# Second layer: skip product on TensorE, y read by ScalarE, the low half of u made by GpSimd and placed by transfers

## The chip, the cores and the metric

The kernel runs on one core of one Trainium2 chip. The metric is the device time of the whole program in microseconds (us); smaller is better. The number to forecast is the median of several runs.

## What is computed

Two layers on an image batch x of shape (4, 128, 64, 64), float32. The first layer is attention over the 4096 pixels with 4 heads, residual and layer norm. The second layer adds three branches of its input: a 3x3 convolution, a linear map in the Fourier plane, and a Mamba block. The change touches the Mamba block alone:

```python
xs = jax.nn.silu((xc + conv1d_b[None, :, None]).transpose(0, 2, 1))
x_dbl = jnp.einsum('bld,rd->blr', xs, x_proj_w)
dt = jax.nn.softplus(jnp.einsum('blr,dr->bld', x_dbl[..., :DT_RANK], dt_proj_w) + dt_proj_b)
...
dA = jnp.exp(dtt[..., None] * A)
h = dA * h + dtt[..., None] * Bt[:, None, :] * xt[..., None]
y = jnp.einsum('bdn,bn->bd', h, Ct)
...
return ys.transpose(1, 0, 2) + x * D
...
y = y * jax.nn.silu(z)
```

There are 256 channels d, 16 states n and 4096 positions l. The last sum, `+ x * D`, is called the skip below, and `dt * xs` is called u.

## The kernel before

`layer0` runs first and writes its result to the DRAM tensor `z_ext`; `layer1` reads it. The engines of `layer1` each run their own list of instructions in order, and semaphores tie them together.

**Tiling.** `layer1` walks over 32 items (4 images x 8 stretches of 512 positions). An item has 32 groups g; a group is 8 channels x 16 states on 128 partitions, over 512 positions. Each engine has an `emit(it, p)` that loops over the groups g of item `it`, and inside each step calls `prepare(it + 1, ...)`, which does a piece of the next item's preparation at a fixed g. So the order is written out by hand by the numbers g.

**One group.** SyncE (SP) loads dt of the group's channels, repeated over the states, into one of 16 buffers `d_a` (L885); ScalarE (ACT) makes the decay exp(dt*A) in it (L1119). TensorE (PE) repeats u over the states with a 0/1 matrix into one of 4 PSUM banks (`repeat_u`, L1021); VectorE (DVE) multiplies this by B (`times_b`, L1181) and runs the recurrence (the scan, L1195) into one of 8 buffers `hh`; ACT keeps the last state (`last_state`, L1112); GpSimd (POOL) multiplies by C into one of 8 buffers `hc` (L1232). After each four groups PE sums the states into the bank of y (`sum_states`, L1004, four matmuls side by side on 32 columns each). Sixteen groups fill one half of y, 128 channels.

**How far the engines may run apart.** PE may do `repeat_u` of group g once scan g - 4 is done, and DVE multiplies it after scan g - 2. ACT makes the decay of group g + 1 after keeping the state of group g - 6. The scan of g waits for POOL's product and ACT's copy of g - 8. Loads of dt run 16 groups ahead.

**y.** DVE reads a finished half of y from PSUM, adds the skip and writes `yt` (`add_skip`, L1166, at g = 21 for half 0 and g = 5 of the next item for half 1). POOL multiplies by the gate (L1215), PE projects (`out_proj`, L1011, at g = 12 and 13), ACT copies the output bank (L1138), DVE adds a row (L1172) and SP stores.

**Preparation of the next item.** TensorE: taps at g = 1 to 7 (L939), `wxd` at 10 and 11, dt at 14 and 15, B and C at 18 and 19, gate at 22 and 23 (L966), the eight products with `wmix` at 29 (L973, L974), and the convolution's products at the g of `FILLS` (L986). ScalarE: softplus pieces at g = 17 to 20. GpSimd: dt's sum at g = 18 (L1220), u at g = 19 (L1223); SP stores dt at its step 16 and reads it back from there. The matmul of u runs in one pass, so u is split: ScalarE copies a rounded high half of 64 partitions into the stack `s_u` (L1064, g = 23 and 24, with the two partition halves one after the other), and DVE writes u minus this into the other 64 partitions (`low`, L1154, g = 23 and 24).

## Time and profile before

| | us |
|---|---|
| median of 3 runs | 5988.45 |
| lowest, highest | 5988.19, 5989.36 |
| the profiled execution, its own time | 5988.07 |
| its span, first to last instruction | 5986.3 |

| engine | busy us | share of the span |
|---|---|---|
| PE (matmul) | 5515.8 | 92% |
| DVE | 4841.2 | 81% |
| POOL | 4207.8 | 70% |
| ACT | 3701.3 | 62% |

How to read it: busy times are sums over both layers, which have different limits, so the second layer has to be read by itself. It fills the time from about 4000 us on. Matmuls overlap in the records, so a busy PE is not a full one. A row of the timeline gives start, duration, engine, line, operation, output and inputs, and in square brackets how long the engine had been idle and who ended that.

### The profile page before, as it was taken

The numbers are of one execution on the slowest core, as the hardware profiler recorded it, in microseconds if no ns is written. First come the engines' busy times: TensorE is split into PE (matmuls) and PEld (weight loads), VectorE is DVE, ScalarE is ACT, GpSimd is POOL, SyncE is SP. The second block draws the span as 40 slices with busy tenths as digits, with TensorE's granted clock in tenths as the row PEclk, the third lists the DMA queues.
The fourth block names the chain that finished last, engine by engine and source line by source line (L and its number), as shares of the span: only waits on it lengthen the run. The fifth ranks groups of instructions, "written<-read, shape, count | busy, mean of one in ns | idle before, by whom it ended". The sixth has DMA issues, their size and how long they took to land. (4 is left out here: it accounts for less than half of the span.)

```text
span 5986.3 us, 84041 instructions
## 1 busy us (share of the span) xinstructions
PE 5515.8 (92%) x27184; PEld 2520.1 (42%) x27184; DVE 4841.2 (81%) x7122; ACT 3701.3 (62%) x7290; POOL 4207.8 (70%) x3213
## 2 busy tenths in 40 slices
PE   7999999999999999999999999968888878888887
PEld 4444444444444444444444444423333333333333
DVE  7777777777777777777777777639999999999999
ACT  3666666665666666666666666656666666666665
POOL 2767666677676677776667776638787887878787
PEclk8999999999999999999999999989999999999999
DMA  4011010110110101101010000024444444454444
GB/s 135 21 43 41 20 38 22 43 40 27 43 35 21 45 20 43 41 24 36 24 26 22 8 22 13 20 94 172 168 161 168 160 169 162 168 168 160 168 160 153
DMA packets 292503, 464.74 MB, mean 78 GB/s; under 512 B 72384, under 2 KB 95808, under 8 KB 290624
## 3 DMA queue, kind: packets, MB, share of 16 engines
q1 hardware_dynamic: 292064, 459.37, 23.6%
q8 instruction: 217, 3.56, 0.2%
q14 instruction: 222, 1.82, 0.1%
HBM read 381.41 MB, written 76.28 MB: 76 GB/s over the span
## 5 line engine op out<-in xcount | busy, mean ns | idle before, releaser
L560 POOL TENSOR_TENSOR sums<-exps 128x512 f32<-128x512 f32 x2048 | 2617.2, 1298 | 1313.2 <-ACT exps L493 1308.3
L569 DVE TENSOR_REDUCE mpart<-ps 128x1 f32<-128x512 f32 x4096 | 2541.6, 683 | 818.9 <-PE ps L369 818.9
L493 ACT ACTIVATE exps<-ps 128x512 f32<-128x512 f32 x4096 | 2127.9, 603 | 1404.0 <-PE ps L376 1403.6
L369 PE MATMUL ps<-k_st,q_ring 96*128 96x512 f32 x4096 | 1753.9, 429 | 17.3 <-DMA k_st<-qk_split 8.9
L1232 POOL TENSOR_TENSOR hc<-hh,c_rep 128x512 f32<-128x512 f32 x1024 | 1361.8, 1338 | 392.3 <-DVE hh L1195 391.9
L376 PE MATMUL ps<-q_ring,k_st 98*128 98x512 f32 x4096 | 1621.7, 397 | 4.0 <-ACT exps L493 3.6
L1195 DVE TENSOR_TENSOR_SCAN hh<-d_a,carry,ps 128x512 f32<-128x512 f32 x1024 | 1308.6, 1281 | 1.0
L369 PEld LDWEIGHTS ps<-k_st,q_ring 96*128 96x128 f32 x4096 | 775.1, 189 | 1063.4 <-DVE mpart L569 508.2
L387 PE MATMUL ps<-exps,v_ring 128*32 128x512 f32 x8192 | 1090.8, 605 | 0.0
L376 PEld LDWEIGHTS ps<-q_ring,k_st 98*128 98x128 f32 x4096 | 777.7, 190 | 148.4 <-ACT exps L493 17.3
L1021 PE MATMUL ps<-s_u,sel_g 128*128 128x512 f32 x1024 | 559.1, 549 | 199.0 <-DVE hh L1195 197.4
L1119 ACT ACTIVATE d_a<-d_a,a_neg 128x512 f32<-128x512 f32 x1024 | 730.8, 720 | 3.6 <-DMA d_a<-dt_dram 2.0
L1181 DVE TENSOR_TENSOR ps<-ps,b_rep 128x512 f32<-128x512 f32 x1024 | 700.8, 687 | 12.6 <-PE ps L1021 11.6
L1021 PEld LDWEIGHTS ps<-s_u,sel_g 128*128 128x128 f32 x1024 | 194.7, 191 | 870.0 <-DVE hh L1195 752.8
L399 PE MATMUL ps<-sums,ones_d 128*32 128x512 f32 x4096 | 533.1, 592 | 0.0
L1004 PE MATMUL ps<-hc,sel_y 128*32 128x512 f32 x2048 | 287.2, 633 | 183.6 <-DVE yt L1166 114.7
L387 PEld LDWEIGHTS ps<-exps,v_ring 128*32 128x32 f32 x8192 | 161.2, 108 | 416.9 <-ACT exps L493 361.2
L1112 ACT COPY carry<-hh 128x1 f32<-128x1 f32 x1024 | 186.7, 183 | 238.8 <-DVE hh L1195 238.5
L939 PE MATMUL ps<-za,wtap 128*128 128x512 f32 x528 | 266.0, 598 | 27.2 <-DMA stage_j<-z_ext 27.2
L986 PE MATMUL ps<-zp,wconv 128*128 128x512 f32 x576 | 290.0, 604 | 0.0
L399 PEld LDWEIGHTS ps<-sums,ones_d 128*32 128x32 f32 x4096 | 133.0, 110 | 306.6 <-issue 298.1
L1064 ACT CAST s_u<-ux 64x1024 fp32r<-64x1024 f32 x66 | 68.9, 1045 | 286.0 <-POOL ux L1223 285.2
(106 smaller groups left out, 3075.4 us busy)
## 6 DMA issues: line engine op xcount, KB each, us to landing
d_a<-dt_dram SPq DMA_DIRECT2D x1040, 256.0 KB
qk_split<-hilo SPq DMA_DIRECT2D x128, 256.0 KB, 2.3
q_ring<-qk_split SPq DMA_DIRECT2D x384, 64.0 KB, 2.0
k_st<-qk_split SPq DMA_DIRECT2D x45, 512.0 KB, 7.1
dt_dram<-dt SPq DMA_DIRECT2D x33, 512.0 KB, 2.8
za<-z_ext SPq DMA_DIRECT2D x33, 320.0 KB, 3.8
zp<-z_ext SPq DMA_DIRECT2D x32, 320.0 KB, 6.6
xc<-in_x SPq DMA_DIRECT2D x32, 256.0 KB, 3.0
```

The costliest lines, as they stand in the source:

```text
L369: nc.tensor.matmul(d_bank(("max", m, t)), q_ring[0:PARTS, m % 4, 128 * i:128 * i + 128], k_st[0:PARTS, g % 2, chunk(kc)], start=True, stop ...
L376: nc.tensor.matmul(a_bank(("exp", n, t)), k_st[0:SHIFT, n // NCH % 2, 128 * t:128 * t + 128], q_ring[0:SHIFT, n % 4, :], start=True, stop= ...
L387: ins = nc.tensor.matmul(ps[D * i:D * i + D, OUT_BANK, :], v_ring[:, n // NCH % 2, 4 * v + i, :], exps[:, (2 * v + i // 2) % 4, CH * (i % ...
L399: nc.tensor.matmul(ps[D * j:D * j + D, DEN_BANK, :], ones_d[:, :], sums[:, u % 8, :], start=(v == 1), stop=(v == QUADS - 1)).then_inc(sum_ ...
L493: nc.scalar.activation(exps[:, u % 4, CH * half:CH * half + CH], a_bank(("exp", n, t)), ACT.Exp, scale=SCALE).then_inc(a_done, 1)
L560: pool.tensor_tensor(sums[:, u % 8, :], exps[:, u % 4, 0:CH], exps[:, u % 4, CH:2 * CH], ALU.add).then_inc(summed, 1)
L569: nc.vector.tensor_reduce(mpart[:, m % 2, t % 4, t // 4:t // 4 + 1], d_bank(("max", m, t)), AX.X, ALU.max).then_inc(d_done, 1)
L1021: nc.tensor.matmul(ps[:, U_BANK + g % NU, :], sel_g[:, j, :], s_u[:, p, s, :], start=True, stop=True).then_inc(u_rep, 1)
L1119: nc.scalar.activation(d_a[:, g % NDA, :], d_a[:, g % NDA, :], ACT.Exp, scale=a_neg[:, s * 8 + j:s * 8 + j + 1]).then_inc(da_ready, 1)
L1181: nc.vector.tensor_tensor(bu, bu, b_rep[:, p, :], ALU.mult).then_inc(bu_ready, 1)
L1195: nc.vector.tensor_tensor_scan(hh[:, g % NHH, :], d_a[:, g % NDA, :], ps[:, U_BANK + g % NU, :], carry[:, it % STEPS, s * 8 + j:s * 8 + j ...
L1232: pool.tensor_tensor(hc[:, g % NHC, :], hh[:, g % NHH, :], c_rep[:, p, :], ALU.mult).then_inc(hc_ready, 1)
```

## The change

In the second layer:

- **Skip.** DVE's `add_skip` is gone. A diagonal matrix of D (`wskip`, loaded once more with the weights) is multiplied with `xs` on PE as the first matmul into the bank of y, in `sum_states` for n = 0 and 4. It opens the accumulation; the sums of states follow.
- **y.** ScalarE copies the finished half from PSUM to `yt` (`read_y`), at g = 23 for half 0 and g = 9 of the next item for half 1, ahead of `prepare` there.
- **Low half of u.** DVE's `low` is gone. ScalarE writes a rounded copy of all of u (`hi_u`) at g = 24 and the two high halves into `s_u` at g = 25. GpSimd subtracts at g = 20 (`lo_u`, 128 partitions). ScalarE's queue issues two transfers at g = 28 (`place_low`) that put the two halves of `lo_u` into the other partitions of `s_u`; TensorE waits for them before g = 0 of the item.
- **dt.** GpSimd's sum of dt is at g = 15 and u at g = 16.
- **Sums of states.** Each moves one group back: g = 9, 13, ..., 29, and 1 and 5 of the next item.

The diff, cut to its core (left out are a rename of a semaphore list, the load of `wskip` as a 16th weight, and the count that waits for it):

```diff
@@ -748,6 +748,9 @@
...
         ux = sb("ux", [128, 2, LC])
+        hi_u = sb("hi_u", [128, 2, LC], F32R)
+        lo_u = sb("lo_u", [128, 2, LC], F32R)
+        wskip = sb("wskip", [128, 2, 128])
@@ -912,6 +915,7 @@
...
+                sp.wait_ge(u_placed, 32 * (NIT + 1))
@@ -1000,9 +1004,10 @@
...
                         ge(pe, y_added, it * 2 + n // 4)
+                        nc.tensor.matmul(ps[:, Y_BANK, :], wskip[:, n // 4, :], xs[:, it % 2, n // 4, :], start=True, stop=False)
...
                         ins = nc.tensor.matmul(ps[32 * i:32 * i + 32, Y_BANK, :], sel_y[:, n % 4, :], hc[:, (4 * n + i) % NHC, :],
-                                               start=(n % 4 == 0), stop=(n % 4 == 3))
+                                               start=False, stop=(n % 4 == 3))
@@ -1015,7 +1020,8 @@
...
                     if g == 0:
-                        pe.wait_ge(lo_ready, it * 2 + 2)
+                        pe.wait_ge(hi_ready, it * 3 + 3)
+                        pe.wait_ge(u_placed, it * 32 + 32)
@@ -1026,7 +1032,7 @@
...
                         prepare(it + 1, 1 - p, g)
-                        if g in (0, 4) and it:
+                        if g in (1, 5) and it:
@@ -1035,7 +1041,7 @@
...
                             fill_g(it, p)
-                        if g >= 8 and g % 4 == 0:
+                        if g >= 9 and g % 4 == 1:
@@ -1058,10 +1064,23 @@
...
-                def high(j, p, stack, src, part):
+                def high(p, part):
...
                     a = slice(64 * part, 64 * part + 64)
-                    nc.scalar.copy(stack[a, p, part::2, :], src[a, :, :]).then_inc(hi_ready, 1)
+                    nc.scalar.copy(s_u[a, p, part::2, :], ux[a, :, :]).then_inc(hi_ready, 1)
+
+                def place_low(j, p):
+
+                    act.wait_ge(lo_ready, j + 1)
+                    for part in range(2):
+                        a, b = slice(64 * part, 64 * part + 64), slice(64 - 64 * part, 128 - 64 * part)
+                        act.dma_start(s_u[b, p, part::2, :].bitcast(F32), lo_u[a, :, :].bitcast(F32)).then_inc(u_placed, 16)
+
+                def read_y(it, half):
+
+                    act.wait_ge(y_done, it * 8 + 4 * half + 4)
+                    ge(act, o_ready, it)
+                    nc.scalar.copy(yt[:, half, :], ps[:, Y_BANK, :]).then_inc(y_added, 1)
@@ -1073,7 +1092,7 @@
...
-                        ge(act, y_added, j * 2 - 2)
+                        ge(act, y_done, j * 8 - 8)
@@ -1094,9 +1113,15 @@
...
                         nc.scalar.copy((b_rep, c_rep)[g - 21][:, p, :], take(j, BI + g - 21)).then_inc(item_read, 1)
-                    elif g in (23, 24):
+                    elif g == 24:
                         act.wait_ge(u_prod, j + 1)
-                        high(j, p, s_u, ux, g - 23)
+                        ge(act, lo_ready, j)
+                        nc.scalar.copy(hi_u[:, :, :], ux[:, :, :]).then_inc(hi_ready, 1)
+                    elif g == 25:
+                        for part in range(2):
+                            high(p, part)
+                    elif g == 28:
+                        place_low(j, p)
@@ -1126,6 +1151,10 @@
...
                             last_state(it - 1, 1 - p, G + g - KEEP)
+                        if g == 23:
+                            read_y(it, 0)
+                        if g == 9 and it:
+                            read_y(it - 1, 1)
@@ -1141,31 +1170,13 @@
...
                         last_state(NIT - 1, 1, g)
+                    read_y(NIT - 1, 1)
...
             def _(dve):
-                def low(j, p, stack, src, part):
-
-                    a, b = slice(64 * part, 64 * part + 64), slice(64 - 64 * part, 128 - 64 * part)
-                    dve.wait_ge(hi_ready, j * 2 + part + 1)
-                    nc.vector.tensor_tensor(stack[b, p, part::2, :], src[a, :, :], stack[a, p, part::2, :].bitcast(F32), ALU.subtract
-                                            ).then_inc(lo_ready, 1)
-
-                def prepare(j, p, g):
-                    if g in (23, 24):
-                        low(j, p, s_u, ux, g - 23)
-
-                def add_skip(it, p, half):
-
-                    dve.wait_ge(y_done, it * 8 + 4 * half + 4)
-
-                    ge(dve, o_ready, it)
-                    nc.vector.scalar_tensor_tensor(yt[:, half, :], xs[:, p, half, :], cols[:, 4 + half:5 + half], ps[:, Y_BANK, :],
-                                                   ALU.mult, ALU.add).then_inc(y_added, 1)
-
@@ -1194,19 +1205,12 @@
...
                                                      carry[:, it % STEPS, s * 8 + j:s * 8 + j + 1], ALU.mult, ALU.add).then_inc(scanned, 1)
-                        prepare(it + 1, 1 - p, g)
-                        if g == 21:
-                            add_skip(it, p, 0)
-                        if it:
-                            if g == 5:
-                                add_skip(it - 1, 1 - p, 1)
-                            if g == 16:
-                                add_row(it - 1, 1 - p)
+                        if g == 16 and it:
+                            add_row(it - 1, 1 - p)
...
                 def tail():
-                    add_skip(NIT - 1, 1, 1)
                     add_row(NIT - 1, 1)
-                steps(prepare, emit, tail)
+                steps(lambda j, p, g: None, emit, tail)
@@ -1215,12 +1219,16 @@
...
                 def prepare(j, p, g):
-                    if g == 18:
+                    if g == 15:
...
                         pool.tensor_tensor(dt[:, :, :], dt[:, :, :], edt[:, :, :], ALU.add).then_inc(dt_sum, 1)
-                    elif g == 19:
+                    elif g == 16:
...
                         pool.tensor_tensor(ux[:, :, :], dt[:, :, :], xs[:, p, :, :], ALU.mult).then_inc(u_prod, 1)
+                    elif g == 20:
+                        pool.wait_ge(hi_ready, j * 3 + 1)
+                        ge(pool, u_placed, j * 32)
+                        pool.tensor_tensor(lo_u[:, :, :], ux[:, :, :], hi_u[:, :, :].bitcast(F32), ALU.subtract).then_inc(lo_ready, 1)
@@ -1288,6 +1296,9 @@
...
                                   i["L1_conv_conv_spatial_b"][:, None], two(i["L1_conv_conv_spectral_b"])], 1))
+    m = np.zeros((128, 2, 128), f)
+    m[p, :, p] = two(i["L1_conv_D"])
+    w["wskip"] = m
```

What the change does to the lists of instructions, at three places. The first is TensorE at g = 24 and 25 (L1021 and L1027 are `repeat_u`, L1004 and L1009 the sum of states, L1007 the skip, L986 and L990 the convolution's products). Before:

```order
L1021 MATMUL ps<-s_u,sel_g 128x512 [waits scanned]
L1004 MATMUL ps<-hc,sel_y 32x512 [waits y_added,hc_ready]
L1004 MATMUL ps<-hc,sel_y 32x512 x3
L1021 MATMUL ps<-s_u,sel_g 128x512 [waits scanned]
L986 MATMUL ps<-zp,wconv 128x512 x2
```

With the change:

```order
L1027 MATMUL ps<-s_u,sel_g 128x512 [waits scanned] x2
L990 MATMUL ps<-zp,wconv 128x512 x2
L1007 MATMUL ps<-xs,wskip 128x512 [waits y_added,hc_ready]
L1009 MATMUL ps<-hc,sel_y 32x512 x4
L1027 MATMUL ps<-s_u,sel_g 128x512 [waits scanned]
```

The sum of states that opens the second half stood at g = 24 alone; it stands at g = 25 now, behind the two products there and with the skip's product ahead of it.

The second is TensorE from g = 28 on (L973, L974, L977 and L978 are the small products with `wmix` of g = 29, L998 the products of g = 30). Before, from g = 28 to the first of the eight small products:

```order
L1021 MATMUL ps<-s_u,sel_g 128x512 [waits scanned]
L1004 MATMUL ps<-hc,sel_y 32x512 [waits hc_ready]
L1004 MATMUL ps<-hc,sel_y 32x512 x3
L1021 MATMUL ps<-s_u,sel_g 128x512 [waits scanned]
L973 MATMUL ps<-wmix,za 128x128 [waits flipped,item_read]
```

With the change, from the last of the eight to g = 31:

```order
L978 MATMUL ps<-wmix,zj 128x128
L1009 MATMUL ps<-hc,sel_y 32x512 [waits hc_ready]
L1009 MATMUL ps<-hc,sel_y 32x512 x3
L1027 MATMUL ps<-s_u,sel_g 128x512 [waits scanned]
L998 MATMUL ps<-hilb,g_t 128x128 x4
L1027 MATMUL ps<-s_u,sel_g 128x512 [waits scanned]
```

The sum stood ahead of the eight small products and now stands behind them, in front of the repeat of g = 30.

The third is ScalarE at g = 23 to 25 (L1119 of before and L1144 of after are the decay, L1112 and L1137 the kept state). Before, g = 23 and 24:

```order
L1119 ACTIVATE d_a<-d_a,a_neg 128x512 [waits dt_in7]
L1112 COPY carry<-hh 128x1 [waits scanned]
L1064 CAST s_u<-ux 64x2x512 [waits u_prod]
L1119 ACTIVATE d_a<-d_a,a_neg 128x512 [waits dt_in8]
L1112 COPY carry<-hh 128x1 [waits scanned]
L1064 CAST s_u<-ux 64x2x512 [waits u_prod]
```

With the change, g = 23 to 25:

```order
L1144 ACTIVATE d_a<-d_a,a_neg 128x512 [waits dt_in7]
L1137 COPY carry<-hh 128x1 [waits scanned]
L1083 COPY yt<-ps 128x512 [waits y_done]
L1144 ACTIVATE d_a<-d_a,a_neg 128x512 [waits dt_in8]
L1137 COPY carry<-hh 128x1 [waits scanned]
L1119 CAST hi_u<-ux 128x1024 [waits lo_ready,u_prod]
L1144 ACTIVATE d_a<-d_a,a_neg 128x512 [waits dt_in9]
L1137 COPY carry<-hh 128x1 [waits scanned]
L1070 CAST s_u<-ux 64x2x512 x2
```

And at g = 27 and 28, with the change:

```order
L1064 ACTIVATE gz<-ps 128x512 [waits item] x2
L1065 ACT_TABLE_LOAD
L1144 ACTIVATE d_a<-d_a,a_neg 128x512 [waits dt_in12]
L1137 COPY carry<-hh 128x1 [waits scanned]
L1077 DMA s_u<-lo_u 64x2x512 [waits lo_ready]
L1077 DMA s_u<-lo_u 64x2x512
L1144 ACTIVATE d_a<-d_a,a_neg 128x512 [waits dt_in13]
```

ScalarE now waits for y at g = 23, makes one more copy of u at g = 24, both high halves at g = 25, and issues two transfers at g = 28.

## Rows read from the trace of the kernel before

**Rows 1.** Windows: us, busy per engine, granted PE clock, DMA share, GB/s.

```profile
4010.00:5972.00 1962.00, 1580.96 (x5613) 640.00 (x5611) 1951.11 (x2203) 1310.55 (x2779) 1580.60 (x1150) 0.97 0.48 166
...
5024.50:5028.00 3.50, 3.50 (x11) 1.51 (x9) 3.50 (x5) 0.00 (x0) 3.50 (x3) 1.00 0.00 0
...
5042.00:5045.50 3.50, 3.50 (x18) 3.50 (x17) 3.50 (x4) 1.04 (x4) 2.55 (x2) 0.50 0.53 204
```

**Rows 2.** Timeline of DVE in one item: starts of scans.

```profile
5010.30 1.28 DVE L1195 TENSOR_TENSOR_SCAN hh<-d_a,carry,ps 128x512 f32<-128x512 f32 x1
...
5012.07 1.28 DVE L1195 TENSOR_TENSOR_SCAN hh<-d_a,carry,ps 128x512 f32<-128x512 f32 x1
...
5028.12 1.29 DVE L1195 TENSOR_TENSOR_SCAN hh<-d_a,carry,ps 128x512 f32<-128x512 f32 x1
...
5030.55 1.30 DVE L1195 TENSOR_TENSOR_SCAN hh<-d_a,carry,ps 128x512 f32<-128x512 f32 x1
...
5032.32 1.30 DVE L1195 TENSOR_TENSOR_SCAN hh<-d_a,carry,ps 128x512 f32<-128x512 f32 x1
...
5035.51 1.28 DVE L1195 TENSOR_TENSOR_SCAN hh<-d_a,carry,ps 128x512 f32<-128x512 f32 x1
...
5038.95 1.27 DVE L1195 TENSOR_TENSOR_SCAN hh<-d_a,carry,ps 128x512 f32<-128x512 f32 x1
```

**Rows 3.** Waits from 4100 to 5900 us: total, times, longest.

```profile
ACT s_u L1064 <- POOL ux L1223: 263.7, 30, 8.8
...
DVE ps L1181 <- PE ps L1021: 6.4, 15, 0.5
```

**Rows 4.** Timeline of PE in the same item as Rows 2.

```profile
5030.20 1.07 PE L1004 MATMUL ps<-hc,sel_y 128*32 128x512 f32 x8 [1.81 <-DVE yt L1166]
5031.20 0.50 PE L1021 MATMUL ps<-s_u,sel_g 128*128 128x512 f32 x1
5031.53 1.88 PE L986 MATMUL ps<-zp,wconv 128*128 128x512 f32 x4
...
5039.49 1.94 PE L1004 MATMUL ps<-hc,sel_y 128*32 128x512 f32 x8 [2.15 <-POOL hc L1232]
5041.36 0.80 PE L1021 MATMUL ps<-s_u,sel_g 128*128 128x512 f32 x1
...
5045.22 0.61 PE L1021 MATMUL ps<-s_u,sel_g 128*128 128x512 f32 x1
```

**Rows 5.** Timeline of PE: repeats of g = 29 and 30 in a later item.

```profile
5900.69 0.50 PE L1021 MATMUL ps<-s_u,sel_g 128*128 128x512 f32 x1
...
5902.73 0.47 PE L1021 MATMUL ps<-s_u,sel_g 128*128 128x512 f32 x1
```

**Rows 6.** Timeline of POOL in the same item as Rows 2.

```profile
5025.41 2.36 POOL L1220 TENSOR_TENSOR dt<-dt,edt 128x1024 f32<-128x1024 f32 x1
5027.73 1.27 POOL L1232 TENSOR_TENSOR hc<-hh,c_rep 128x512 f32<-128x512 f32 x1
...
5031.28 4.72 POOL L1232 TENSOR_TENSOR hc<-hh,c_rep 128x512 f32<-128x512 f32 x3
```

**Rows 7.** Timeline of ACT in the same item as Rows 2.

```profile
5006.38 0.58 ACT L1079 COPY xd<-ps 128x512 f32<-128x512 f32 x1
...
5031.35 1.05 ACT L1064 CAST s_u<-ux 64x1024 fp32r<-64x1024 f32 x1 [8.79 <-POOL ux L1223]
...
5040.12 0.72 ACT L1119 ACTIVATE d_a<-d_a,a_neg 128x512 f32<-128x512 f32 x1
```

**Rows 8.** Timeline of SP: issues; the second is dt's store.

```profile
5008.07 11.19 SPq L885 DMA_DIRECT2D d_a<-dt_dram  x7
5027.80 0.37 SPq L879 DMA_DIRECT2D dt_dram<-dt  x1
```

**Rows 9.** Part 6 of the page: transfers, count, size, us to landing.

```profile
dt_dram<-dt SPq DMA_DIRECT2D x33, 512.0 KB, 2.8
```

More of the change, by code:

```diff
@@ L760, in layer1 @@
             "loaded1", "mixed", "a_exp", "carry_zero", "row_zero", "halved")]
-        NLOAD = 15 * 16
+        NLOAD = 16 * 16
         with nc.Block() as block:
@@ L770, in _ @@
                         (wconv[:, :, :], w["wconv"]), (wspec[:, :, :], w["wspec"]), (hilb[:, :], w["hilb"]),
-                        (hil0[:, :], w["hil0"].to_broadcast([128, W])), (wout[:, :, :], w["wout"]), (cols[:, :], w["cols"]),
+                        (hil0[:, :], w["hil0"].to_broadcast([128, W])), (wout[:, :, :], w["wout"]), (cols[:, :], w["cols"]), (wskip[:, :, :], w["wskip"]),
                         (a_neg[:, :], w["a_log"])):
@@ L815, in layer1 @@
          u_rep, da_ready, bu_ready, scanned, kept, hc_ready, y_done, y_added, gated, z_used, o_ready, o_copied,
-         o_full, o_even, o_odd, dt_stored) = [sem(x) for x in (
+         o_full, o_even, o_odd, dt_stored, u_placed) = [sem(x) for x in (
              "z_in", "zp_in", "flipped", "item", "item_read", "sp_log", "dt_sum", "u_prod",
              "hi_ready", "lo_ready", "u_rep", "da_ready", "bu_ready", "scanned", "kept", "hc_ready", "y_done",
-             "y_added", "gated", "z_used", "o_ready", "o_copied", "o_full", "o_even", "o_odd", "dt_stored")]
+             "y_added", "gated", "z_used", "o_ready", "o_copied", "o_full", "o_even", "o_odd", "dt_stored", "u_placed")]
         dt_in = [sem(f"dt_in{i}") for i in range(NDA)]
```

## The prediction

> **What bounds the kernel now.** I read the windows first. From 4010 to 5972 us, where the second layer's 32 items run, VectorE is busy for 1951 of 1962 us and every other engine is well below [rows 1]. An item takes 1962 / 32 = 61.3 us. The chain of waits on the page names GpSimd, but GpSimd is busy for only 1581 us of this stretch [rows 1]; it is named because it often stands between two steps of VectorE. The list of waits settles it: the only idle time of VectorE in 1800 us is 6.4 us for TensorE [rows 3]. So what leaves VectorE's list in this layer leaves the time, until something else is late. The first layer is not touched.
>
> The timeline of VectorE gives the price of each piece, as the distance from scan to scan. A plain group takes 5012.07 - 5010.30 = 1.77 us. The group with the skip takes 2.43, so the skip costs 0.66. The groups with the two subtractions for u take 3.19 and 3.44, so these cost 1.42 and 1.67 [rows 2]. I use these distances and not durations, because neighbours overlap by about 0.1 us.
>
> **What goes away.** Per item: two skips, 2 x 0.66 = 1.32; two subtractions, 3.09; together 4.41 us. The floor left is 32 x 1.77 = 56.6 plus the small row addition, about 0.1. Adding 4.41 to 56.7 gives 61.1; the measured 61.3 has 0.2 more, which is the wait for TensorE (15 times 0.4 over 29 items, [rows 3]). 32 x 4.41 = 141 us.
>
> **The wait for TensorE.** It stands at g = 30. TensorE may repeat u of a group once the scan four back is done, and VectorE wants it two scans later, 3.54 us. The repeat takes 0.5, so TensorE may be 3.0 us late at a step. In the item shown it waited 2.15 us for GpSimd at g = 28, ran on at granted clock 0.50 (the 1.2 GHz level), and needed 5045.22 - 5041.36 = 3.86 us for the step g = 29 [rows 1, 4]. At full clock the same step took 2.04 us [rows 5] and nothing waited. The change makes that wait shorter for three reasons. The sum of states that waits moves one group back. The dt sum and u leave GpSimd three groups earlier. And GpSimd's products get faster: alone one takes 1.27 us, but three took 4.72, 1.57 each, while VectorE's subtraction ran beside them [rows 6].
>
> **What TensorE gets.** Each item has two more products for the skip, a shape that costs 1.88 / 2 = 0.94 us, so 1.9 us on top of 1581 / 32 = 49.4 busy [rows 1, 4]: 51.3 of 56.7. That fits on the mean, so the crowded place decides, g = 25 to 29. Starts give a repeat 0.33 and a sum of states 1.00 [rows 4]. g = 25 holds repeat, two products, skip and sum, 0.33 + 3 x 0.94 + 1.00 = 4.15; g = 26 one product, 1.27; g = 27 two, 2.21; g = 28 only the repeat, 0.33; g = 29 is 2.04 at full clock plus the sum that now stands there, 3.04. Sum 11.0 us against 5 x 1.77 = 8.85. TensorE is 2.15 us late at g = 30, under the 3.0 allowed: no stall at full clock. The waits of 1.8 us for the skip [rows 4] also go, since ScalarE reads y early (below). So I expect the 6.4 us of waits to go too, 7 us over 32 items. I give back 2 us for an item or two at half clock.
>
> **GpSimd.** It gets one subtraction of 128 x 1024. The same shape costs 2.36 us for dt [rows 6]. Against that, products beside VectorE's subtractions fall from 1.57 to about 1.27, some six per item, 1.8 us. Its sum is near 49.4 + 0.6 = 50 of 56.7 us. Its worst place is g = 15 to 22: three operations of 2.36 and a gate of 1.27, 8.35 us, on top of eight products, 8 x 1.24 = 9.9, in 8 x 1.77 = 14.2 us. It falls about 4.1 us behind after g = 22. The scan needs GpSimd only eight groups back, 14 us. The sum of states at g = 29 needs group 23, which GpSimd ends 4.1 + 1.3 = 5.4 us after scan 23. TensorE starts g = 29 after scan 25 and is 0.9 us late there, so it reaches that sum 3.54 + 0.9 + 2.04 = 6.5 us after scan 23: a margin of 1 us, and another 0.85 us up to the 3.0 allowed. The early dt sum needs ScalarE's softplus of g = 20; ScalarE makes that right after scan 14, while GpSimd comes there 1.3 us after scan 15.
>
> The Trainium skill, SBUF — State Buffer, section "Who interferes with whom", says that a VectorE instruction with two inputs in SBUF contends with a GpSimd instruction that reads SBUF, by a lock that fully blocks the other. The 1.57 against 1.27 us agrees [rows 6]. By that rule the scan and the product with B, each with one input in PSUM, are not touched by the new subtraction. Its page Perfetto Trace Analysis, section "Optimizing Scalar/DVE Operations", speaks against the change: offloading between these two engines might not help.
>
> **ScalarE.** New per item: one more copy of u, 1.05; two copies of y, 0.58 each [rows 7]; two issues, for which SP's 0.37 is the nearest row [rows 8]. Together 2.9 us on 1311 / 32 = 41 [rows 1]. What matters is that a decay is never later than its scan. At g = 23 ScalarE waited 8.79 us for u and then needed 5040.12 - 5031.35 = 8.8 us to the decay of g = 28 [rows 7]. Now it waits there for y instead: TensorE may start g = 21 after scan 17 and needs 0.33 + 1.88 + 1.00 = 3.2 us. Then 0.6 for y, 8.8 as before, 1.0 for the new copy, 0.7 for the decay: 14.3 us after scan 17. The decay of g = 28 is wanted ten groups after it, at 17.7. Margin 3.4 us, so nothing of this shows. At g = 9 it reads y right after scan 3, before its old wait for VectorE.
>
> **Transfers.** The low halves add 0.5 MB per item. They are issued about 15 us after scan 17, so near scan 26, and TensorE wants them after scan 28 for use after scan 31. A transfer of the same 512 KB landed in 2.8 us [rows 9]; at half the 204 GB/s that a crowded stretch moved [rows 1] it is 5 us. Wanted at the latest after 9 us: hidden. SP gains: it issued nothing from 5019 to 5027.8 while it waited for dt [rows 8], and the DMA stood at 0 [rows 1]. Now dt is there about 5 us sooner.
>
> **Ends.** Before the first item nothing hides the new steps. The extra copy puts 1.0 us into ScalarE's chain, and the transfers come after its gate; TensorE's eight products cover some 2 of their 2.8 to 5 us. I take 3.5, bounds 1.5 and 6. The sixteenth weight load is 128 KB among 15, 0 to 1 us, taken as 0.5. At the end a ScalarE copy of 0.58 takes the place of VectorE's 0.7: nothing.
>
> **Sum.** Against the profiled execution, 5988.1 (the median is 0.4 higher): 5988.1 - 141.1 - 7 + 2 + 3.5 + 0.5 = 5846.
>
> **Rivals.**
>
> *TensorE late at g = 30.* If the half clock stays, sum and products of g = 29 take 1.87 + 3.86 = 5.73 instead of 3.04 [rows 4]. The lag becomes 4.8 us, 1.8 over. In half of the items, as now, 29 us: 5875; in all of them 58: 5904. For it speaks that the sum moved in front of the tightest repeat; against it, that the waits of 1.8 and 2.15 us which came before the low clock mostly go. Chance 0.15.
>
> *ScalarE, GpSimd or the transfers late somewhere.* An issue on ScalarE could cost 2 us instead of 0.4 and eat the margin of 3.4; the sum at g = 29 could wait on GpSimd by 1 or 2 us. Each us that reaches VectorE once an item costs 32 us: 5870 to 5940. Chance 0.11.
>
> *GpSimd's subtraction blocks VectorE.* If it held back a scan for its 2.36 us in each item, 32 x 2.36 = 76 us come back: 5922. Against it: dt's sum runs beside scans that take 1.29 and 1.30 instead of 1.28 [rows 2, 6]. Chance 0.03.
>
> *The DMA becomes the bound, and it ends slower.* The stretch moves 166 GB/s [rows 1], so 61.3 x 166 = 10.2 MB per item, 10.7 with the placed halves. At 204 GB/s that takes 52.5 us of 56.7. From 189 GB/s down the loads of dt set the pace, and below 10.7 / 61.3 = 175 GB/s the item is longer than before. At 168 it is 63.7 us: 5988 + 32 x 2.4 = 6065. For it: crowded stretches hold 204 and no more, and two queues now interleave. Against it: the DMA stands still for several us of each item now. The Trainium skill, DMA: Bandwidth & Descriptors, section "Issuing engines are not separate DMA queues", says that transfers of all issuers run on the same 16 engines, so a second queue adds no room. Chance 0.04.
>
> *The gain is not delivered.* Some other wait keeps the item at 60 us or above, for example a chain through `u_placed`: 5945 to 5990. Chance 0.02.
>
> **How the numbers follow.** The forecast, 5838 to 5858, has 0.65. The range 5838 to 5885 takes in the forecast and the half-clock case in half of the items, and a part of the late suppliers, about 0.8. A measurement of this kernel tells 0.2%, 12 us, from no change. Faster: 0.94. Within 0.2%: 0.01. Slower: 0.05.
>
> **What would show it.** In the profile after, VectorE's list holds only scans, products with B and row additions; scans are 1.77 us apart at every g, and an item takes 56.8 us. Waits of VectorE for TensorE stay under 10 us; if they stand at g = 30 with 1 to 2 us each and the clock at half, the first rival is right. Idle before a scan that ends with ScalarE or a transfer is the second. GpSimd's products take 1.27 at every g. A DMA share that is flat near 0.53 and 204 GB/s, with decays waiting for loads, is the DMA case. ScalarE's wait at g = 23 falls from 8.8 to about 3 us.

## The result, and the profile after

The kernel became faster, but only by half of the forecast, and the time lies outside the predicted range.

| | us |
|---|---|
| before, median of 4 runs | 5988.32 |
| after, median of 4 runs | 5921.32 (5914.82 to 5924.34) |
| ratio | 0.9887, 95% interval 0.9870 to 0.9904 |
| the profiled execution of after, its own time | 5914.82 |
| forecast, range | 5846, 5838 to 5885 |

The profiled execution fell by 5988.07 - 5914.82 = 73.25 us, where 142 were forecast. The window of the second layer comes first, with the columns of [rows 1]: length, then busy us (and instructions) of TensorE, its weight loads, VectorE, ScalarE and GpSimd, then clock, DMA share and GB/s.

```profile
4010.00:5890.00 1880.00, 1617.10 (x5710) 650.60 (x5711) 1870.16 (x2070) 1379.73 (x2864) 1581.95 (x1177) 0.96 0.55 181
```

VectorE (DVE) is busy for 1870 of 1880 us, as before. An item now takes 58.8 us and not 56.8. So the bound is still VectorE's own list, with 2 us more in it than it should hold. The groups of that list, by line (busy us, mean ns, idle before them and who ended it), are first those of after and then the small row addition of before. Of the 46.0 us of idle time at L1192, 41.8 are the wait before the first item.

```profile
L1206 DVE TENSOR_TENSOR_SCAN hh<-d_a,carry,ps 128x512 f32<-128x512 f32 x1024 | 1293.7, 1266 | 0.0
L1192 DVE TENSOR_TENSOR ps<-ps,b_rep 128x512 f32<-128x512 f32 x1024 | 685.0, 672 | 48.6 <-PE ps L1027 46.0
L1183 DVE TENSOR_TENSOR o_sb<-o_sb,row 128x64 f32<-128x64 f32 x31 | 63.9, 2062 | 0.0
```

```profile
L1172 DVE TENSOR_TENSOR o_sb<-o_sb,row 128x64 f32<-128x64 f32 x31 | 6.7, 217 | 0.0
```

The subtractions and skips are gone. But an instruction on 64 columns, the same before and after, went from 217 to 2062 ns, more than nine times as long: 57 us over the layer. The timelines of VectorE and GpSimd (POOL) in one item of after show what stands beside it:

```profile
5042.77 1.27 DVE L1206 TENSOR_TENSOR_SCAN hh<-d_a,carry,ps 128x512 f32<-128x512 f32 x1
5043.96 0.67 DVE L1192 TENSOR_TENSOR ps<-ps,b_rep 128x512 f32<-128x512 f32 x1
5044.54 1.27 DVE L1206 TENSOR_TENSOR_SCAN hh<-d_a,carry,ps 128x512 f32<-128x512 f32 x1
5045.73 2.08 DVE L1183 TENSOR_TENSOR o_sb<-o_sb,row 128x64 f32<-128x64 f32 x1
5047.73 0.69 DVE L1192 TENSOR_TENSOR ps<-ps,b_rep 128x512 f32<-128x512 f32 x1
5048.33 1.26 DVE L1206 TENSOR_TENSOR_SCAN hh<-d_a,carry,ps 128x512 f32<-128x512 f32 x1
```

```profile
5045.36 2.36 POOL L1224 TENSOR_TENSOR dt<-dt,edt 128x1024 f32<-128x1024 f32 x1
5047.69 1.26 POOL L1240 TENSOR_TENSOR hc<-hh,c_rep 128x512 f32<-128x512 f32 x1
```

The addition starts 0.37 us after GpSimd's sum of dt and ends at 5047.81, 0.09 us after that sum ends at 5047.72. It doesn't wait for a result of it: it adds a row to the output of the item before. In the profile it counts as busy, so no view of idle time shows this wait. The change had moved dt's sum from g = 18 to g = 15, and GpSimd comes to it just as VectorE comes to the row addition behind scan 16.

**A ledger of the steps.** A plain step from scan to scan takes 1.769 us (5042.77 to 5044.54 above). For each kernel I added up what each step between two scans takes beyond that, over 32 items, from the starts in the timeline of VectorE. A step is named by the scan that ends it, and items are counted from 0; the last column is the experiment `e1_row13` below.

| step, and what stands in it | before | after | e1 |
|---|---|---|---|
| 6 and 22: skips (before) | 41.4 | 0 | 0 |
| 24 and 25: subtractions (before) | 99.1 | 0 | 0 |
| row addition (step 17; in e1 14) | 4.2 | 62.1 | 4.2 |
| 29: wait for TensorE's repeat of g = 30 | 8.7 | 0 | 0 |
| 1, 21, 25: late repeats of TensorE | 0 | 11.1 | 0 |
| rest | -0.9 | 0.1 | 0.6 |
| sum | 152.5 | 73.3 | 4.8 |
| first scan starts at | 4008.64 | 4014.22 | 4015.62 |

The sum of after is 79.2 us lower; the layer starts 5.6 later, and 0.35 lies elsewhere: 5988.07 - 79.2 + 5.95 = 5914.8.

**What follows from the held addition.** The 11.1 us in the steps 1, 21 and 25 are four waits of VectorE for TensorE, 0.6 to 1.3 us each, and many steps that are 0.1 to 0.2 us longer. Two of the four waits, and some 9 of the 11.1 us, lie in steps 21 and 25. One of these two items (item 3), timelines of TensorE (PE) and VectorE, then the windows of it:

```profile
4219.28 1.02 PE L990 MATMUL ps<-zp,wconv 128*128 128x512 f32 x2
4222.71 0.80 PE L1027 MATMUL ps<-s_u,sel_g 128*128 128x512 f32 x1 [2.41 <-DVE hh L1206]
4223.31 3.62 PE L990 MATMUL ps<-zp,wconv 128*128 128x512 f32 x4
...
4229.26 0.70 DVE L1192 TENSOR_TENSOR ps<-ps,b_rep 128x512 f32<-128x512 f32 x1 [1.29 <-PE ps L1027]
```

```profile
4218.00:4220.00 2.00, 1.59 (x5) 0.49 (x3) 2.00 (x2) 1.60 (x4) 2.00 (x2) 1.00 0.54 198
...
4223.40:4227.00 3.60, 3.60 (x9) 1.07 (x11) 3.60 (x5) 0.00 (x0) 3.60 (x4) 0.50 0.18 62
```

While the addition is held, TensorE has no scan to follow and stands still for 2.41 us. Behind that the granted clock is 0.50, the 1.2 GHz level, the two products of g = 21 (x4 records) take 3.62 us where two took 1.88 [rows 4], and the repeat for g = 22 comes 1.29 us late. I read the granted clock in the six microseconds after scan 17 of every item. In after it is below 1.00 in 19 of the 32 items, and all the extra time at steps 21 and 25 lies in these 19; in the other 13 both steps are plain. In e1, where nothing is held, it is 1.00 in all 32.

These 13 items are not like the 19. Item 0 has no row addition. In the other 12 the granted clock had fallen to the lower level 2.7 to 3.9 us before scan 16, ahead of the hold, and was back at the start of that scan or shortly behind it; TensorE had more work left when the hold came and stood still for only 1.62 to 1.70 us, against 2.40 to 2.42 in each of the 19. Item 7 is one of the 12, with scan 16 at 4454.22:

```profile
4450.57 1.86 PE L990 MATMUL ps<-zp,wconv 128*128 128x512 f32 x2
...
4459.31 0.50 PE L1027 MATMUL ps<-s_u,sel_g 128*128 128x512 f32 x1 [1.62 <-DVE hh L1206]
4459.65 1.88 PE L990 MATMUL ps<-zp,wconv 128*128 128x512 f32 x4
```

```profile
4451.00:4454.00 3.00, 3.00 (x10) 0.20 (x8) 3.00 (x4) 3.00 (x6) 2.02 (x3) 0.50 0.53 199
```

Why the clock falls early in some items stays open: it does so in 10 items of e1 as well, without a held addition.

The 2.1 us at step 1 have another source. The two waits there stand at the start of items 12 and 20, behind a wait of TensorE for the placing transfers:

```profile
4719.12 0.70 PE L1027 MATMUL ps<-s_u,sel_g 128*128 128x512 f32 x2 [2.84 <-DMA s_u<-lo_u]
```

The granted clock is 0.66 in the five microseconds from there, and the repeat for g = 2 comes 0.6 us late; in item 20 the wait for the transfers is 3.09 us and the repeat 1.0 us late.

The runs of after spread over 9.5 us. Those of before spread over 3.7 in this set and over 7.1 in a later set of 13, so it is not shown that the held addition makes the spread.

The other readings of after, in the order of the prediction. Waits from 4100 to 5850 (total us, times, longest), the page's part 6 (count, size, us to landing), and ScalarE (ACT) at g = 23 of one item:

```profile
ACT yt L1083 <- PE ps L1009: 124.9, 30, 6.0
...
SPq L882 <- POOL dt L1224: 92.4, 30, 3.1
...
PE ps L1027 <- DMA s_u<-lo_u: 37.9, 25, 3.1
```

```profile
s_u<-lo_u ACTq DMA_DIRECT2D x66, 256.0 KB, 6.1
```

```profile
5052.93 0.59 ACT L1083 COPY yt<-ps 128x512 f32<-128x512 f32 x1 [3.11 <-PE ps L1009]
```

### The profile page after: what moved, and what is told of

Same layout as the page of the kernel before. It is cut to its first block and busy times, and to the rows that moved or that the text cites. A ratio compares the mean times of both kernels' runs of the same rounds, so it can differ in the third digit from the quotient of the medians.

```text
span 5913.0 us, 84431 instructions
## 1 busy us (share of the span) xinstructions
PE 5552.9 (94%) x27312; PEld 2531.2 (43%) x27312; DVE 4763.0 (81%) x6992; ACT 3774.8 (64%) x7387; POOL 4221.5 (71%) x3246
## 5 line engine op out<-in xcount | busy, mean ns | idle before, releaser
L1240 POOL TENSOR_TENSOR hc<-hh,c_rep 128x512 f32<-128x512 f32 x1024 | 1296.5, 1279 | 294.8 <-DVE hh L1206 288.4
L1206 DVE TENSOR_TENSOR_SCAN hh<-d_a,carry,ps 128x512 f32<-128x512 f32 x1024 | 1293.7, 1266 | 0.0
L1027 PE MATMUL ps<-s_u,sel_g 128*128 128x512 f32 x1024 | 569.4, 567 | 264.9 <-DVE hh L1206 219.7
L1144 ACT ACTIVATE d_a<-d_a,a_neg 128x512 f32<-128x512 f32 x1024 | 732.8, 721 | 3.0 <-DMA d_a<-dt_dram 1.3
L1192 DVE TENSOR_TENSOR ps<-ps,b_rep 128x512 f32<-128x512 f32 x1024 | 685.0, 672 | 48.6 <-PE ps L1027 46.0
L1027 PEld LDWEIGHTS ps<-s_u,sel_g 128*128 128x128 f32 x1024 | 193.6, 190 | 862.8 <-DVE hh L1206 689.6
L1137 ACT COPY carry<-hh 128x1 f32<-128x1 f32 x1024 | 188.3, 184 | 310.8 <-DVE hh L1206 310.8
L990 PE MATMUL ps<-zp,wconv 128*128 128x512 f32 x576 | 315.7, 652 | 0.0
L1009 PE MATMUL ps<-hc,sel_y 128*32 128x512 f32 x2048 | 297.7, 656 | 4.8 <-POOL hc L1240 4.8
L580 DVE COPY den_parts<-ps 128x512 f32<-128x512 f32 x128 | 88.5, 692 | 138.2 <-PE ps L399 138.2
```

The lines of the kernel that those rows point to most:

```text
L1027: nc.tensor.matmul(ps[:, U_BANK + g % NU, :], sel_g[:, j, :], s_u[:, p, s, :], start=True, stop=True).then_inc(u_rep, 1)
L1144: nc.scalar.activation(d_a[:, g % NDA, :], d_a[:, g % NDA, :], ACT.Exp, scale=a_neg[:, s * 8 + j:s * 8 + j + 1]).then_inc(da_ready, 1)
L1192: nc.vector.tensor_tensor(bu, bu, b_rep[:, p, :], ALU.mult).then_inc(bu_ready, 1)
L1206: nc.vector.tensor_tensor_scan(hh[:, g % NHH, :], d_a[:, g % NDA, :], ps[:, U_BANK + g % NU, :], carry[:, it % STEPS, s * 8 + j:s * 8 + j ...
L1240: pool.tensor_tensor(hc[:, g % NHC, :], hh[:, g % NHH, :], c_rep[:, p, :], ALU.mult).then_inc(hc_ready, 1)
```

## Experiments

The theory: the row addition, with two inputs in SBUF, can't run beside a GpSimd instruction on SBUF and is held until that ends; all else of the forecast stands. Each ratio below is to runs of before taken beside the experiment, with medians from 5986.1 to 5989.4 us. The rivals: the new skips and transfers slow VectorE in some other way; or the order of GpSimd's work is what costs, and the early sum of dt was a mistake.

**1. The row addition three groups earlier, where GpSimd has only its products.**

```diff
-                        if g == 16 and it:
+                        if g == 13 and it:
                             add_row(it - 1, 1 - p)
```

> The changed kernel with VectorE's row addition moved from g = 16 to g = 13, nothing else. Theory: at g = 16 the row addition (two inputs in SBUF) is held up by GpSimd's sum of dt, 2.06 us instead of 0.22, 31 times, 57 us in all. At g = 13 GpSimd runs only products, so the addition takes 0.2 us again and the time falls by 57 us, from 5921 to about 5864, items of 56.9 us. Rival: something else lengthens it, for example its input from ScalarE or the denser traffic of the new schedule; then it stays at 2 us at g = 13 and the time stays near 5921.

Measured: 5849.06 us (5846.79 to 5850.33), ratio to before 0.9769, interval 0.9752 to 0.9785. One number in the code brings back 72 us, 15 more than expected. The same two engines there:

```profile
5003.69 1.27 DVE L1206 TENSOR_TENSOR_SCAN hh<-d_a,carry,ps 128x512 f32<-128x512 f32 x1
5004.88 0.20 DVE L1183 TENSOR_TENSOR o_sb<-o_sb,row 128x64 f32<-128x64 f32 x1
5005.00 0.69 DVE L1192 TENSOR_TENSOR ps<-ps,b_rep 128x512 f32<-128x512 f32 x1
```

```profile
5003.27 1.28 POOL L1240 TENSOR_TENSOR hc<-hh,c_rep 128x512 f32<-128x512 f32 x1 [0.49 <-DVE hh L1206]
5005.04 1.28 POOL L1240 TENSOR_TENSOR hc<-hh,c_rep 128x512 f32<-128x512 f32 x1 [0.49 <-DVE hh L1206]
```

GpSimd's product ends at 4.55 and the next starts at 5.04; the addition, 4.88 to 5.08, fits into the gap. VectorE's waits for TensorE from 4100 to 5780 us are 0.3 us in all, and steps 21 and 25 are plain. So the 9 us of late repeats there hung on the held addition too. The 2.1 us at step 1 are 0.6 here, but they come back as 2.1 in experiment 8, where nothing is held either, so they don't hang on it. The ledger of e1 is 68.5 us below that of after, 57.9 for the addition and nearly all of the rest for the repeats; the medians differ by 72. The windows, with an item of 56.8 us:

```profile
4010.00:5830.00 1820.00, 1592.64 (x5748) 643.80 (x5748) 1815.23 (x2078) 1387.62 (x2875) 1581.27 (x1181) 0.98 0.56 188
```

**2. The row addition left at g = 16, but with one input in PSUM.**

```diff
-                    nc.vector.tensor_tensor(o_sb[:, p, 0:W], o_sb[:, p, 0:W], row0[:, it % STEPS, :], ALU.add).then_inc(o_full, 1)
+                    dve.wait_ge(bu_ready, min((it + 1) * G + 18, NIT * G))
+                    nc.vector.tensor_tensor(o_sb[:, p, 0:W], ps[:, U_BANK + 1, 0:W], row0[:, it % STEPS, :], ALU.add).then_inc(o_full, 1)
```

> The changed kernel with the row addition left at g = 16, but with its first input read from a PSUM bank instead of from the output tile in SBUF, so the first 64 columns of each output stretch are not the ones computed; 64 columns and the wait on ScalarE's copy stay. Theory (a lock on what both engines read from SBUF, taken by two SBUF inputs): with one SBUF input it takes about 0.25 us beside the sum of dt, and the time is about 5864. Rival (any VectorE instruction that lands beside a 1024-column GpSimd instruction, or one that writes to SBUF, is held up): it stays at 2 us and 5921.

This kernel leaves the output itself out of the first 64 columns of each output stretch. Measured: 5847.42 us (5845.97 to 5847.49), ratio 0.9765 (0.9751 to 0.9780), 17 us below what was expected. The group by line, in the second layer, then one addition and its neighbour on GpSimd:

```profile
L1184 DVE TENSOR_TENSOR o_sb<-ps,row 128x64 f32<-128x64 f32 x31 | 6.8, 218 | 0.0
```

```profile
5008.58 0.23 DVE L1184 TENSOR_TENSOR o_sb<-ps,row 128x64 f32<-128x64 f32 x1
```

```profile
5008.24 2.35 POOL L1225 TENSOR_TENSOR dt<-dt,edt 128x1024 f32<-128x1024 f32 x1
```

Same place, same wait on the copy of the output, same neighbour on GpSimd, which started 0.34 us before the addition and ran on long after it: 218 ns. What held the addition was its two inputs in SBUF, neither its place in the order nor a semaphore. The Trainium skill, SBUF — State Buffer, section "Who interferes with whom", states that a VectorE instruction with two SBUF inputs contends with a GpSimd instruction that reads SBUF, and that one with at most one SBUF input does not. The runs agree with it: 0.22 us with an input in PSUM, 2.06 without.

**3. The kernel before, with dt's sum and u three groups earlier and nothing else.**

```diff
-                    if g == 18:
+                    if g == 15:
...
-                    elif g == 19:
+                    elif g == 16:
```

> The kernel before with one part of the change alone: the sum of dt at g = 15 and u at g = 16 on GpSimd. Theory: the row addition at g = 16 meets the sum of dt here too and takes 2.06 us, 31 x 1.84 = 57 us, less up to 8 us for the waits on TensorE at g = 30 that an earlier u may remove: 6037 to 6046. Rival (the lengthening needs the new transfers or copies of the changed kernel): 5980 to 5990.

Measured: 6050.97 us (6049.45 to 6052.42), ratio 1.0106 (1.0091 to 1.0121): 64 us slower than before, 5 above the expected range. Its groups, from a stretch that ends at 5990 us, before the last of the 31 additions:

```profile
L1172 DVE TENSOR_TENSOR o_sb<-o_sb,row 128x64 f32<-128x64 f32 x30 | 62.1, 2071 | 0.0
...
L1154 DVE TENSOR_TENSOR s_u<-ux,s_u 64x1024 fp32r<-64x1024 f32 x64 | 97.7, 1527 | 31.0 <-ACT s_u L1064 29.1
```

This part of the change alone, without the new copies and transfers, makes the loss at the addition: 58.2 us in the ledger, as in after. It doesn't make the late repeats: TensorE stands still for 1.43 us beside each hold here, and its granted clock in the six microseconds after scan 17 is 1.00 in all 32 items. It also costs 64 x (1527 - 1359) ns = 11 us in the subtractions, which have two inputs in SBUF as well and now meet GpSimd's products in another phase.

**4. The kernel before, with the skip on TensorE and y copied by ScalarE, and nothing else.**

```diff
+                        nc.tensor.matmul(ps[:, Y_BANK, :], wskip[:, n // 4, :], xs[:, it % 2, n // 4, :], start=True, stop=False)
...
+                        if g == 23:
+                            read_y(it, 0)
+                        if g == 9 and it:
+                            read_y(it - 1, 1)
...
-                        if g == 21:
-                            add_skip(it, p, 0)
...
-                            if g == 5:
-                                add_skip(it - 1, 1 - p, 1)
```

> The kernel before with one part of the change alone: the skip as a product on TensorE and y read by ScalarE at g = 23 and g = 9; u, dt and the sums of states as before. Theory (each skip was worth 0.66 us of VectorE's list): 63 x 0.66 = 42 us off, 5946. Rival (TensorE or ScalarE becomes late by it, since u still comes at g = 19): less than half of it, above 5967.

Measured: 5964.69 us (5963.74 to 5966.81), ratio 0.9962 (0.9947 to 0.9977). 22 us faster than before by the medians and 24 by the profiled executions, little more than half of 2 x 32 x 0.66 = 42. That lies between the theory's 5946 and the rival's 5967, and the rival's cause, a late TensorE or ScalarE, isn't what the ledger shows: no step but that of the first subtraction grew. Both skips are gone from VectorE, but the first subtraction behind the place of one takes longer. The timelines there, and then the same subtraction of before, whose neighbours on GpSimd are in [rows 6]:

```profile
5020.06 1.27 DVE L1208 TENSOR_TENSOR_SCAN hh<-d_a,carry,ps 128x512 f32<-128x512 f32 x1
5021.36 1.88 DVE L1167 TENSOR_TENSOR s_u<-ux,s_u 64x1024 fp32r<-64x1024 f32 x1
...
5023.88 1.28 DVE L1208 TENSOR_TENSOR_SCAN hh<-d_a,carry,ps 128x512 f32<-128x512 f32 x1
```

```profile
5019.65 4.72 POOL L1239 TENSOR_TENSOR hc<-hh,c_rep 128x512 f32<-128x512 f32 x3
```

```profile
5033.65 1.22 DVE L1154 TENSOR_TENSOR s_u<-ux,s_u 64x1024 fp32r<-64x1024 f32 x1
```

The step takes 3.82 us where it took 3.19 [rows 2], and the ledger has 20.3 us more at this step than before: the half that is missing (some 5 us of waits for TensorE also went). VectorE now reaches the subtraction 0.66 us earlier against GpSimd's products, and spends the time inside it. With products 1.23 us apart and 1.27 long, an estimate from these rows, the second of the three ends 0.13 us after the subtraction starts in before (5033.78 against 5033.65) and 0.79 us after it in this kernel (5022.15 against 5021.36): 0.66 us more, which is what the subtraction grew by. That this is the same mutual exclusion is argued from the two timelines; experiment 2 shows the exclusion only for the row addition.

**5. Kernel e1 with the skip back on VectorE** (`add_skip` at g = 21 and 5, no product on TensorE, no copy on ScalarE).

```diff
-                        nc.tensor.matmul(ps[:, Y_BANK, :], wskip[:, n // 4, :], xs[:, it % 2, n // 4, :], start=True, stop=False)
...
+                        if g == 21:
+                            add_skip(it, p, 0)
+                        if g == 5 and it:
+                            add_skip(it - 1, 1 - p, 1)
-                        if g == 16 and it:
+                        if g == 13 and it:
```

> The changed kernel with the row addition at g = 13, and the skip given back to VectorE at g = 21 and g = 5 (one input in SBUF, one in PSUM), without the product on TensorE and without ScalarE's reading of y. So it is the u part, the dt part and the shifted sums alone. Theory (a skip is worth its own 0.66 us when no two-input instruction of VectorE stands behind it): 63 x 0.66 = 42 us above 5849, 5891. Rival (the skip is cheap and the kernel with the skip alone gained 22 us because that is what a skip is worth, 0.35 us each): 5871.

Measured: 5887.57 us (5886.98 to 5890.72), ratio 0.9835 (0.9820 to 0.9850), 38.5 us more than e1. The ledger has 20.4 and 21.1 at the two steps, 41.5, the 0.66 us each of [rows 2]. Where no subtraction stands on VectorE behind it, the skip is worth its full price. So the same 42 us of skips were worth 22 in one kernel and 38.5 in the other, and the parts of the change can't be priced one by one and added.

**6 and 7. Other places for the row addition**, to see whether its price can be told beforehand from where GpSimd stands: g = 20 and g = 22 in place of 16.

```diff
-                        if g == 16 and it:
+                        if g == 20 and it:
```

> The changed kernel with the row addition at g = 20. There GpSimd works off short products of 1.24 us back to back. In the trace with the row at g = 13, scan 20 ends at 5017.40 and the product then running ends at 5018.31. Theory (VectorE's two-input instruction waits for whatever GpSimd instruction is running, of any length): the row addition takes about 1.0 us, 31 x 0.8 = 25 us above 5849: 5874. Rival (only instructions of 1024 columns hold it up): 0.2 us and 5849.

Measured: 5874.74 us (5873.09 to 5875.95), ratio 0.9808 (0.9792 to 0.9824), as expected. The addition and what GpSimd does beside it:

```profile
5033.07 1.02 DVE L1183 TENSOR_TENSOR o_sb<-o_sb,row 128x64 f32<-128x64 f32 x1
```

```profile
5031.50 4.97 POOL L1240 TENSOR_TENSOR hc<-hh,c_rep 128x512 f32<-128x512 f32 x4
```

Four products back to back, 1.24 us apart: the third starts at 5031.50 + 2.48 = 5033.98. The addition comes at 5033.07 and ends at 5034.09. It waits for the end of the running product, no longer; all 31 additions take 1.00 to 1.03 us.

> The changed kernel with the row addition at g = 22. There GpSimd runs the new subtraction: in the trace with the row at g = 13, scan 22 ends at 5020.94 and the subtraction runs from 5020.76 to 5023.14. Theory (the wait goes by what GpSimd runs at that moment, which instruction it is does not matter): the row addition takes 2.2 to 2.3 us, 31 x 2.1 = 65 us above 5849, 5914, plus up to 10 us for TensorE falling idle. Rival (it is particular to the sum of dt): 0.2 us and 5849. SP's store of the output stretch waits 4 groups longer here, which both theories hold to be hidden.

Measured: 5926.63 us (5917.38 to 5930.79), ratio 0.9893 (0.9878 to 0.9908), some 12 us over the 5914 that was expected and 3 beyond the 10 us that were allowed on top. In 28 items the addition takes 2.24 to 2.29 us, what is left of `lo_u`, as expected. In three it takes 6, which makes 3 x 3.7 = 11 of the 12 us:

```profile
4410.65 5.95 DVE L1183 TENSOR_TENSOR o_sb<-o_sb,row 128x64 f32<-128x64 f32 x1
```

```profile
4410.45 2.39 POOL L1231 TENSOR_TENSOR lo_u<-ux,hi_u 128x1024 fp32r<-128x1024 f32 x1
4412.77 2.53 POOL L1240 TENSOR_TENSOR hc<-hh,c_rep 128x512 f32<-128x512 f32 x2
4415.22 1.30 POOL L1219 TENSOR_TENSOR yt<-yt,gz 128x512 f32<-128x512 f32 x1
4418.47 1.27 POOL L1240 TENSOR_TENSOR hc<-hh,c_rep 128x512 f32<-128x512 f32 x1 [1.95 <-DVE hh L1206]
```

Here VectorE did not get its turn when `lo_u` ended. It waited through three more instructions of GpSimd and got on at 4416.60, when GpSimd ran out of work at 4416.52. So "until the instruction ends" is the usual case and not the worst. The three can't be told from the others by how the two engines meet: the addition starts 0.17 to 0.21 us after `lo_u` in all 31.

**8. Kernel e1, with 4 of the 16 loads of dt before the placing transfers of the first item and 12 behind them.**

```diff
-                for g in range(NDA):
+                for g in range(4):
+                    load_dt(0, 0, g)
+                sp.wait_ge(u_placed, 32)
+                for g in range(4, NDA):
                     load_dt(0, 0, g)
```

> The changed kernel with the row addition at g = 13, and before the first item SP loads only 4 of the 16 repeats of dt, waits for the two placing transfers of u's low half, and then loads the other 12. In the trace of the kernel with the row addition at g = 13 the first product with B starts at 4014.42 us, after TensorE waited 5.27 us for the placing transfers, which ran against those loads. Theory (the two streams share the transfer engines, and the placing lands after about 3 us alone): first product with B near 4009.5, time 4 to 5 us below the 5849 of row13 alone, about 5845. Rival (the placing takes as long alone, it is its own latency): first product with B unchanged, 5849 or more.

Measured: 5847.17 us (5846.20 to 5848.28), ratio 0.9763 (0.9748 to 0.9777): 2 us below e1, inside the spread of both. TensorE starts 9.6 us after the issue of the first placing transfer, where it took 10.4 in e1 but 9.6 in after as well, and it still waited for them, 4.26 us (5.27 in e1, 4.25 in after). So holding back these 12 loads doesn't make the first pair land sooner, and the expected gain isn't shown. The pairs for items 1 to 3 of this run, though, landed 4.4 to 5.0 us after issue, and all others after 9 us and more. What sets this time stays open.

**9. The kernel after, with dt's sum and u back at g = 18 and 19.** This asks for the other half of the question: was moving dt wrong?

```diff
-                    if g == 15:
+                    if g == 18:
...
-                    elif g == 16:
+                    elif g == 19:
```

> The changed kernel with one part undone: the sum of dt back at g = 18 and u at g = 19, the row addition left at g = 16. Theory: the row addition meets only a short product again and takes 0.2 us, so the 57 us and the idle of TensorE behind it go; but u comes three groups later, ScalarE's decay of g = 28 then ends about 1 us after it is wanted, 32 us: between 5849 and 5885. Rival (the early dt was needed as a whole, the delays through u's chain cost more than the collision): 5921 or above.

Measured: 5980.55 us, median of 10 runs (5975.88 to 5989.21), ratio 0.9991 (0.9982 to 1.0001). All of the gain is gone, though the row addition is back at 0.20 us: the theory said 5849 to 5885 and was wrong, and the rival, 5921 or above, was right. I had counted only ScalarE's chain to the decay of g = 28. The timelines of one item (ScalarE and its queue, TensorE, VectorE), then the windows:

```profile
5029.72 1.04 ACT L1119 CAST hi_u<-ux 128x1024 fp32r<-128x1024 f32 x1 [4.42 <-POOL ux L1227]
...
5036.35 0.60 ACTq L1077 DMA_DIRECT2D s_u<-lo_u  x1
...
5045.82 1.19 PE L1027 MATMUL ps<-s_u,sel_g 128*128 128x512 f32 x2 [4.24 <-issue]
...
5046.63 1.30 DVE L1192 TENSOR_TENSOR ps<-ps,b_rep 128x512 f32<-128x512 f32 x2 [1.09 <-PE ps L1027]
...
5051.35 0.70 DVE L1192 TENSOR_TENSOR ps<-ps,b_rep 128x512 f32<-128x512 f32 x1 [2.25 <-PE ps L1027]
```

```profile
5035.00:5042.00 7.00, 5.18 (x37) 3.44 (x35) 6.43 (x8) 6.94 (x14) 7.00 (x7) 1.00 0.69 197
5046.00:5052.00 6.00, 6.00 (x16) 2.15 (x16) 3.13 (x5) 2.42 (x7) 3.24 (x3) 0.56 0.53 199
```

u comes late, so the rounded copy, the subtraction and the placing transfers do too; they are issued at 5036.35 and TensorE can start on the next item only at 5045.82, 9.5 us later. It has then been idle for 4.24 us and goes on at a granted clock of 0.56. The ledger has 45.6 us more than before at step 0, 65.9 at step 1, and 21.2 at step 28, the one term that I had counted, at 32. So the early dt is needed in this kernel; that the addition stood beside it was the mistake.

## Why the prediction was wrong, point by point

**The step that failed** is in "What goes away": "the floor left is 32 x 1.77 = 56.6 plus the small row addition, about 0.1". The duration was read in a place where GpSimd left it alone, and kept, although the change moved a 2.36 us instruction of GpSimd onto it. It measured 2.06 us: 57.9 us more over the layer than at its old length, and some 9 more through the late repeats behind it. With the 2.1 at step 1 that is 69 us, and the profiled execution lies 68.8 above the forecast. The other terms nearly cancel against their forecasts: 2.0 more for the head and the end, 0.6 for skips and subtractions and 1.0 for the rest of the ledger, and 3.7 less for the waits at g = 30. The median lies 6.5 higher still. The part on GpSimd had what was needed. It states that the lock holds for VectorE instructions with two inputs in SBUF, and that GpSimd comes to dt's sum 1.3 us after scan 15; by the timeline above that is just before VectorE comes to the addition. But it tests the rule on the scan and the product with B only and on the new subtraction only, not on the third instruction of the list and the moved sum.

**What held.** In e1, which is the change without the collision, each term can be read:

- Skips and subtractions: 141.1 forecast, 140.5 in the ledger.
- The waits for TensorE at g = 30: 7 forecast with 2 given back; 8.7 went, and 0.6 is left at other places.
- The head: 3.5 forecast, bounds 1.5 to 6, and 0.5 for the weight load; 5.6 measured in after and 7.0 in e1. Counted from GpSimd's first u, and so without what comes before it, it is 5.5 and 6.4. The estimate was low, since the transfers that it rests on took 9 to 10 us from issue at this place and not 2.8 to 5.
- The sum: 5846 forecast; e1's profiled execution took 5847.9, its median 5849.06.
- GpSimd, in after: its products take 1.28 us on the mean and its new subtraction 2.37. SP's longest wait for dt is 3.1 us.
- ScalarE at g = 23: forecast about 3 us of waiting; 2.7 to 3.1 in every item of e1. In after, the row shown above (3.11) is one of the short ones, the mean is 124.9 / 30 = 4.2 and the longest 6.0. A queue issue took 0.61 us on the median and not 0.37, which the margin of 3.4 us covers.

**Landed on the wrong row.** Transfers: 6.1 us on the median of the page, estimate 2.8 to 5 [rows 9]. TensorE waits for them in 25 items, up to 3.1 us, and VectorE's lead covers that in all but two of them; there the 2.1 us at step 1 follow. The conclusion "hidden" nearly held, with less room than claimed, as experiment 9 shows.

**The rivals.** "GpSimd's subtraction blocks VectorE" gave 5922, and 5921 was measured. That it is so near is luck: its price of 76 us stands against 58 for the held addition, 9 and 2 for late repeats and 6.5 between the profiled execution and the median. What it had right is one GpSimd instruction of 2.36 us in the way once an item. The mechanism was another: not the new subtraction but the moved sum, and not a scan but the small addition. Its chance of 0.03 rested on the argument that scans aren't touched, which is true and was beside the point. The case of a half clock that costs at g = 30 did not occur; the lower clock did come, behind the held addition in 19 items, and it cost at steps 21 and 25. DMA was no bound: 181 to 188 GB/s, with next to no waits of the decays for their loads.

## What to carry to other kernels

When work moves on GpSimd, list every VectorE instruction with two inputs in SBUF, however small, and set it against the new timeline of GpSimd. Its price is, in most items here, what is left of the instruction beside it, and its own duration is nearly nothing; put it into a gap of GpSimd, or give it an input in PSUM. Such a wait stands in the busy time, so compare the mean duration of each unchanged line between two profiles before looking at idle times.

## What the runs showed of the hardware

- VectorE held behind GpSimd usually goes on when the running instruction ends: 2.06, 1.02 and 2.25 us in three places. In 3 of 31 items of one kernel it did not, and waited 5.97 us until GpSimd had nothing left to do. What decides this stays open.
- A gain can vanish into what looks like the same exclusion: 42 us of skips taken from VectorE's list gave 22, because the next instruction with two SBUF inputs took 1.88 instead of 1.22 us. That the exclusion is the reason is argued, not shown.
- A transfer of 256 KB from SBUF to SBUF landed in 6.1 us on the median of the page. TensorE could start 9 to 10 us after the issue of the first of a pair, at the start and in experiment 9; three pairs of experiment 8 landed in 4.4 to 5.0 us.
- Once an item, TensorE had nothing to do beside the held addition. In the 19 items where that took 2.40 to 2.42 us, the granted clock was at the lower level behind it; in the 12 where it took 1.62 to 1.70 us it was not, and there the clock had been low just before. A short hold of VectorE thus came back as a second, smaller loss some groups later. The length of the idle time alone doesn't tell: at the start of an item of e1, the granted clock of the next three microseconds was 0.60 behind 1.92 us of waiting in one item and 1.00 behind 2.57 in another.
- The fastest versions measured are e1, 5849 us, and e1 with the loads behind the placing, 5847: 2.3% below the kernel before.
